# A perceiver block's key tiles on one core: a second buffer for the normed tiles, a batch's first and last tile normed by halves, and another order at a batch's turn

## The reference, cut to what matters

```python
kvx = jnp.einsum('bsi,oi->bso', cond, w_kv_x)       # cond: 8 batches x 1601 rows x 512
kx, vx = jnp.split(kvx, 2, axis=-1)
kx = _ln(kx.reshape(b, sc, g, d), kxln_w, kxln_b)   # g = 8 heads of d = 128, normed each by itself
...
xout = _gqa(qx, kx, vx).reshape(b, s, nh * d)       # softmax(q k^T / sqrt(d)) v
```

## Time and profile before

| | us |
|---|---|
| median of 3 runs | 2889.55 (2889.37 to 2892.36) |
| profiled execution, its time | 2885.77 |
| profiled execution, its span | 2884.0 |
| TensorE busy in the span | 2675.9 (93%) |
| VectorE busy | 1785.2 (62%) |
| ScalarE busy | 1506.5 (52%) |
| GpSimd busy | 465.2 (16%) |
| mean granted TensorE clock | 0.976 |

### The profile page before, as it was taken

How to read it: one execution, slowest core, us unless ns; L and a number is a source line. 1 busy time by engine, 2 the same in 40 slices (tenths; PEclk the granted TensorE clock), 3 DMA queues, 4 the chain that set the end, 5 groups by cost and what they waited for, 6 DMA issues and landing times.

```text
span 2884.0 us, 38434 instructions
## 1 busy us (share of the span) xinstructions
PE 2675.9 (93%) x13446; PEld 2168.4 (75%) x13446; DVE 1785.2 (62%) x4725; ACT 1506.5 (52%) x2919; POOL 465.2 (16%) x376
## 2 busy tenths in 40 slices
PE   6889999999999999999999999989998888969999
PEld 4777787787787787786786777868876778747887
DVE  6748437347356356365374375668668785557997
ACT  6946326235235244244253253446775567846776
POOL 3402002002011011011020020014332222011111
PEclk9999999999999999999999999999999999989999
DMA  3442012021021030030020021435666532529996
GB/s 121 132 154 74 4 45 74 4 60 59 4 71 48 5 89 24 6 94 11 20 85 4 24 86 32 137 117 163 162 183 185 150 76 57 187 90 387 375 372 235
DMA packets 238815, 303.07 MB, mean 105 GB/s; under 512 B 127641, under 2 KB 156953, under 8 KB 225313
## 3 DMA queue, kind: packets, MB, share of 16 engines
q1 hardware_dynamic: 235824, 296.36, 32.3%
q0 software_dynamic: 2800, 4.27, 0.6%
HBM read 259.48 MB, written 46.98 MB: 106 GB/s over the span
## 4 chain that ended last, share of the span: by engine, by line
PE 76%; DVE 11%; ACT 6%; DMA 2%; issue 2%; SPq 1%; POOL 1%; POOLq 0%; DVEq 0%; ACTq 0%
PE ps L103 19%; PE ps L105 19%; PE ps L104 19%; PE ps L753 5%; PE ps L735 3%; PE ps L772 3%; PE ps L802 2%; DVE lnw L1977 1%; DVE zz L1980 1%; DVE cv L1944 1%; PE ps L793 1%; DVE lnw L850 1%; POOL lnw L1099 1%; DMA ca<-cat_d 1%; PE ps L385 1%
## 5 line engine op out<-in xcount | busy, mean ns | idle before, releaser
L1099 POOL TENSOR_TENSOR lnw<-lnw,half 128x8 f32<-128x8 f32 (+1 forms) x104 | 170.9, 1643 | 1417.7 <-DVE lnw L855 1417.7
L103 PE MATMUL ps<-cnh,pth 128*128 128x512 f32 (+1 forms) x832 | 331.8, 399 | 13.6 <-ACT kn L981 13.6
L103 PE MATMUL ps<-whf,cth 128*128 128x512 f32 (+1 forms) x832 | 334.8, 402 | 0.0
L105 PE MATMUL ps<-whf,ctl 128*128 128x512 f32 (+1 forms) x832 | 326.3, 392 | 0.0
L105 PE MATMUL ps<-cnh,ptl 128*128 128x512 f32 (+1 forms) x832 | 326.0, 392 | 0.0
L104 PE MATMUL ps<-cnl,pth 128*128 128x512 f32 (+1 forms) x832 | 325.7, 391 | 0.0
L104 PE MATMUL ps<-wlf,cth 128*128 128x512 f32 (+1 forms) x832 | 325.6, 391 | 0.0
L981 ACT ACTIVATE pr<-ps,lnw 128x128 f32<-128x128 f32 (+1 forms) x384 | 144.2, 456 | 163.8 <-DVE lnw L874 163.8
L2418 DVE TENSOR_TENSOR ml<-mr,mh 128x2048 fp32r<-128x2048 f32 x90 | 203.4, 2287 | 32.2 <-ACT mh L2362 32.2
L971 DVE TENSOR_SCALAR pc<-ps,sm 128x512 f32<-128x512 f32 x64 | 48.1, 751 | 282.1 <-PE ps L105 282.1
L1043 ACT ACTIVATE xo<-ps 128x128 f32<-128x128 f32 x64 | 17.7, 277 | 371.0 <-PE ps L802 371.0
(11 more groups left out here) (331 smaller groups left out, 6086.1 us busy)
## 6 DMA issues: line engine op xcount, KB each, us to landing
mr<-in_moe SPq DMA_DIRECT2D x90, 1024.0 KB, 6.6
ctr<-in_ctxt SPq DMA_DIRECT2D x96, 256.0 KB, 2.9
pr<-in_ctxn SPq DMA_DIRECT2D x96, 256.0 KB
wr<-in_wqkv SPq DMA_DIRECT2D x64, 256.0 KB, 2.9
wvf<-in_wattn SPq DMA_DIRECT2D x12, 1024.0 KB, 4.8
ca<-cat_d SPq DMA_DIRECT2D x16, 512.0 KB, 4.2
qk_d<-cv SPq DMA_DIRECT2D x32, 256.0 KB, 3.2
wr<-in_wz SPq DMA_DIRECT2D x32, 256.0 KB, 3.3
```

The lines of the kernel that those rows point to most:

```text
L103: pe.matmul(dst, lh, rh, start=first, stop=False)
L105: return pe.matmul(dst, ll, rh, start=False, stop=last)
L1099: po.tensor_tensor(rs[0:w, s, :], nv[0:w, s, :], half[0:w, 0:8], ALU.pow).then_inc(kx_rs, 1)
```

## The change

The even tiles of a batch (0, 2, ... 12) are now normed into kn0 and the odd ones into kn (kn_of), and a tile waits for the turn of the tile two before it, tile 0 for that of the last batch's tile 12. Tiles 0 and 12 get their statistics, GpSimd's root and minus mean times root in two halves of four heads: the first half when part 0 of their projection is done (a new semaphore, kx_half), the second when all of it is. In a turn the first four transposes wait for ScalarE's norm alone and the last four for VectorE's.

The lists at a batch's turn are laid anew. TensorE turns tile 10 between the two parts of tile 12's projection; multiplies the first two score pieces before it turns tile 11; projects two chunks of the next tile's part 0, the third score piece, turns tile 12, projects the other two chunks, the last score piece, and part 1. VectorE norms tile 10 ahead of tile 11's statistics, then tile 12's first half of statistics, tile 11's norm, tile 12's second half; the next tile 0's first half of statistics stands before the first reciprocal of the softmax. ScalarE norms tile 12 ahead of writing tile 11's keys.

```diff
+        def in_halves(n):
+            return n % 13 in (0, 12)
+        def kx_half_of(n):
+            return 2 * (n // 13) + 1 + n % 13 // 12
+        def kx_stat_of(n, h):
+            b, i = divmod(n, 13)
+            return 15 * b + (1 + h if i == 0 else i + 2 + (h if i == 12 else 0))
+        def kn_of(n):
+            return kn if n % 13 % 2 else kn0
...
@@ kx_pe @@
                 elif i == 0:
                     pe.wait_ge(kn_ac, n)
-                    pe.wait_ge(kn_dv, n)
...
             for part in parts:
+                if part == 1 and i == 0 and b > 0:
+                    pe.wait_ge(kn_dv, n)
...
+                if part == 0 and chunks[-1] == 3 and in_halves(n):
+                    f.then_inc(kx_half, 1)
@@ kx_turn_pe @@
-            src = kn if i else kn0
-            pe.wait_ge(kn_ac, n + 1)
-            pe.wait_ge(kn_dv, n + 1)
+            src = kn_of(n)
             for p in range(2):
+                pe.wait_ge((kn_ac, kn_dv)[p], n + 1)
@@ s3_pe @@
-                    kx_pe(pe, n)
+                    kx_pe(pe, n, (0,))
+                    if i == 12:
+                        kx_turn_pe(pe, n - 2)
+                    kx_pe(pe, n, (1,))
...
-                    if i > 1:
+                    if 1 < i < 12:
                         kx_turn_pe(pe, n - 2)
+                score_pe(pe, b, 0, 0)
+                score_pe(pe, b, 0, 1)
                 kx_turn_pe(pe, 13 * b + 11)
-                for w in range(3):
-                    score_pe(pe, b, 0, w)
+                if b + 1 < NB:
+                    kx_pe(pe, 13 * b + 13, (0,), (0, 1))
+                score_pe(pe, b, 0, 2)
                 kx_turn_pe(pe, 13 * b + 12)
                 if b + 1 < NB:
-                    kx_pe(pe, 13 * b + 13, (0,), (0, 1))
+                    kx_pe(pe, 13 * b + 13, (0,), (2, 3))
                 score_pe(pe, b, 0, 3)
                 if b + 1 < NB:
-                    kx_pe(pe, 13 * b + 13, (0,), (2, 3))
                     kx_pe(pe, 13 * b + 13, (1,))
@@ kn_free @@
             if i == 0 and b > 0:
-                eng.wait_ge(k_turned, 2 * (n - 13) + 2)
+                eng.wait_ge(k_turned, 2 * (n - 1) + 2)
             elif i == 1 and b > 0:
-                eng.wait_ge(k_turned, 2 * (n - 2) + 2)
                 eng.wait_ge(p_turned, 32 * b - 4)
             elif i > 1:
-                eng.wait_ge(k_turned, 2 * (n - 1) + 2)
+                eng.wait_ge(k_turned, 2 * (n - 2) + 2)
@@ new, called by kx_norm_dv and by the lists @@
+        def kx_nmr_dv(dv, n):
+            dv.wait_ge(kx_rs, kx_stat_of(n, 0))
+            dv.scalar_tensor_tensor(nmr[0:w, s, 0:4], mv[0:w, s, 0:4, 0], -1.0, rs[0:w, s, 0:4],
+                                    ALU.mult, ALU.mult).then_inc(kx_nm, 1)
@@ s3_dv @@
+                    if i == 12:
+                        kx_norm_dv(dv, n - 2)
                     if i > 1:
                         kx_stats_dv(dv, n - 1)
-                    if i > 2:
+                    if 2 < i < 12:
                         kx_norm_dv(dv, n - 2)
-                    split_ctxn_dv(dv, n - 1)
+                    if i < 12:
+                        split_ctxn_dv(dv, n - 1)
...
+                kx_stats_dv(dv, 13 * b + 12, (0,))
                 kx_norm_dv(dv, 13 * b + 11)
-                kx_stats_dv(dv, 13 * b + 12)
+                kx_nmr_dv(dv, 13 * b + 12)
+                kx_stats_dv(dv, 13 * b + 12, (1,))
+                split_ctxn_dv(dv, 13 * b + 11)
                 kx_norm_dv(dv, 13 * b + 12)
...
+                if b + 1 < NB:
+                    kx_stats_dv(dv, 13 * b + 13, (0,))
                 t_rinv = {0: rinv_dv(dv, b, 0)}
                 split_ctxn_dv(dv, 13 * b + 12)
...
                     if g == 0 and b + 1 < NB:
-                        kx_stats_dv(dv, 13 * b + 13)
+                        kx_stats_dv(dv, 13 * b + 13, (1,))
+                        kx_nmr_dv(dv, 13 * b + 13)
@@ s3_ac @@
                 kx_norm_ac(ac, 13 * b + 11)
+                kx_norm_ac(ac, 13 * b + 12)
                 k_out_ac(ac, 13 * b + 11)
-                kx_norm_ac(ac, 13 * b + 12)
                 k_out_ac(ac, 13 * b + 12)
@@ s3_po @@
+                if in_halves(n):
+                    for h in range(2):
+                        po.wait_ge(kx_var, kx_stat_of(n, h))
+                        po.tensor_tensor(rs[0:w, s, 4 * h:4 * h + 4], nv[0:w, s, 4 * h:4 * h + 4], half[0:w, 0:4],
+                                         ALU.pow).then_inc(kx_rs, 1)
```

More of the change, by code:

```diff
@@ L606, in s1b_ac @@
             self_out_ac(ac, 7)
+        kx_half = sem("kx_half")
         kx_done, kx_var, kx_rs, kx_nm = sem("kx_done"), sem("kx_var"), sem("kx_rs"), sem("kx_nm")
@@ L842, in s3_pe, with kx_stats_dv @@
                         xo_pe(pe, m - 1)
-        def kx_stats_dv(dv, n):
+        def kx_stats_dv(dv, n, halves=(0, 1)):
             b, i = divmod(n, 13)
             w, s = TILES[i][1], i % 4
+            lo, hi = 4 * halves[0], 4 * halves[-1] + 4
             src = bank(KSET[i], 2)[0:w, :]
-            dv.wait_ge(kx_done, n + 1)
-            for g in range(8):
+            if halves == (0,):
+                dv.wait_ge(kx_half, kx_half_of(n))
+            else:
+                dv.wait_ge(kx_done, n + 1)
+            for g in range(lo, hi):
                 t = vs(dv.bn_stats(bns[0:w, s, g, :], src[:, 128 * g:128 * g + 128]))
             dv.wait_ge(dv_step, t)
-            for g in range(8):
+            for g in range(lo, hi):
                 t = vs(dv.bn_aggr(mv[0:w, s, g, :], bns[0:w, s, g, :]))
             dv.wait_ge(dv_step, t)
-            dv.tensor_scalar(nv[0:w, s, :], mv[0:w, s, :, 1], 1e-5, None, ALU.add).then_inc(kx_var, 1)
+            dv.tensor_scalar(nv[0:w, s, lo:hi], mv[0:w, s, lo:hi, 1], 1e-5, None, ALU.add).then_inc(kx_var, 1)
         def kn_free(eng, n):
@@ L860, in kn_free @@
             if i == 0 and b > 0:
-                eng.wait_ge(k_turned, 2 * (n - 13) + 2)
+                eng.wait_ge(k_turned, 2 * (n - 1) + 2)
             elif i == 1 and b > 0:
-                eng.wait_ge(k_turned, 2 * (n - 2) + 2)
                 eng.wait_ge(p_turned, 32 * b - 4)
             elif i > 1:
-                eng.wait_ge(k_turned, 2 * (n - 1) + 2)
+                eng.wait_ge(k_turned, 2 * (n - 2) + 2)
+        def kx_nmr_dv(dv, n):
+            i = n % 13
+            w, s = TILES[i][1], i % 4
+            dv.wait_ge(kx_rs, kx_stat_of(n, 0))
+            dv.scalar_tensor_tensor(nmr[0:w, s, 0:4], mv[0:w, s, 0:4, 0], -1.0, rs[0:w, s, 0:4],
+                                    ALU.mult, ALU.mult).then_inc(kx_nm, 1)
         def kx_norm_dv(dv, n):
@@ L871, in kx_norm_dv @@
             src = bank(KSET[i], 2)[0:w, :]
[L872 to L875, removed]
+            dst = kn_of(n)
+            if not in_halves(n):
+                kx_nmr_dv(dv, n)
+            dv.wait_ge(kx_rs, kx_stat_of(n, 1))
             kn_free(dv, n)
@@ L916, in s3_dv @@
         def s3_dv(dv):
-            kx_stats_dv(dv, 0)
+            kx_stats_dv(dv, 0, (0,))
+            kx_stats_dv(dv, 0, (1,))
             split_ctxt_dv(dv, 2)
@@ L923, in s3_dv @@
             dv.wait_ge(self_o, 8)
+            kx_nmr_dv(dv, 0)
             kx_norm_dv(dv, 0)
@@ L976, in kx_norm_ac @@
             src = bank(KSET[i], 2)[0:w, :]
-            dst = kn if i else kn0
+            dst = kn_of(n)
             ac.wait_ge(kx_nm, n + 1)
@@ L1097, in s3_po @@
                 w, s = TILES[n % 13][1], n % 13 % 4
-                po.wait_ge(kx_var, n + 1)
-                po.tensor_tensor(rs[0:w, s, :], nv[0:w, s, :], half[0:w, 0:8], ALU.pow).then_inc(kx_rs, 1)
+                if in_halves(n):
[3 more added lines that the diff above has]
+                                         ALU.pow).then_inc(kx_rs, 1)
+                else:
+                    po.wait_ge(kx_var, kx_stat_of(n, 1))
+                    po.tensor_tensor(rs[0:w, s, :], nv[0:w, s, :], half[0:w, 0:8], ALU.pow).then_inc(kx_rs, 1)
         x = sb("x", [128, 4, 512])
@@ L2025, in program @@
         o_high, o_low, gr_silu = Again(self_exp, 8), Again(self_p, 8), Again(self_turned, 8)
-        og_out, og_turned, gated = Again(kx_var, 104), Again(kx_rs, 104), Again(kx_nm, 104)
+        og_out, og_turned, gated = Again(kx_var, 120), Again(kx_rs, 120), Again(kx_nm, 104)
         ot_high, ot_low, out_done = Again(kx_done, 104), Again(kn_ac, 104), Again(kn_dv, 104)
```

## The result

| | before | after |
|---|---|---|
| median, us | 2890.95 (2889.37 to 2894.64, 4 runs) | 2852.74 (2850.96 to 2854.01, 4 runs) |
| ratio | | 0.9866 (95% interval 0.9848 to 0.9883) |
| profiled execution's span, us | 2884.0 | 2850.2 |

The change makes the kernel 38.2 us faster by the medians, 1.3%. Forecast were 38.6 us and a time of 2851.

The account below looks back on a forecast made before the run. TensorE, busy 93% of the span, bounds the kernel, so only its waits could be won: 33.4 (seven turns) + 2.7 (batch 7) + 2.5 (clock) = 38.6 us off 2889.55, forecast 2851, range 2843 to 2869.

Parts of the forecast that it names:

- The place: Stage 3: TensorE's winnable waits stand at a batch's turn; the second buffer gives nothing in the steady loop.
- The sum of a turn: Tile 12's first matmul to first p v: 21.95 us in place of 26.72, 4.77 less, seven times 33.4.
- The half root: GpSimd's root of half a tile, 4 columns, in a batch's turn: taken as 1.06 us, range up to 1.64.
- The row of 4 columns: GpSimd's root of 4 columns in another stage's trace, 1060 ns, taken as the half root's price.
- the rival at 1.64: A half root costs 1.64 us, as much as 8 columns; 3.57 a turn, time 2859; chance 0.10.
- The first wait: TensorE's wait of 2.50 us before tile 11's turn, laid to the single buffer for normed tiles.
- the wait moves: Only the buffer's 2.50 us a turn goes, later chains end as late: 20 us, time 2869.5; chance 0.12.
- Batch 7: Last batch's turn, without a next tile to fill with: p's transposes at 15.35 for 18.07, 2.7 us less.
- The clock: Shorter TensorE waits mean fewer low-clock stretches: 2.5 us saved of about 5, bounds 0 and 5.
- The slower rival: The clock falls more often, with four more low stretches a turn 8 us slower, 2897; chance 0.03.
- The base: Start of the sum: profiled execution 2885.77 us, giving 2847.2; median 3.8 higher, 2889.55, giving 2851.

Follow-up runs that it names:

- e5: Changed kernel with VectorE's low half of tile 11's context moved behind the norm of tile 12: 2851.62 us, ratio 0.986 to the kernel before.
- e1: Kernel before with only the second buffer for normed tiles added: 2884.17 us, ratio 0.9974 to the kernel before.
- e4: Changed kernel with tile 10's turn put back behind tile 12's whole projection: 2866.73 us, ratio 0.9903 to the kernel before.
- e2: Changed kernel with tiles 0 and 12 normed whole again, not in halves: 2924.62 us, ratio 1.0116 to the kernel before.
- e6: Changed kernel with VectorE's low half of tile 12's context moved behind the next tile 0's norm: 2844.81 us, ratio 0.9836 to the kernel before.
- e3: Changed kernel with one buffer again for tiles 1 to 12: 2867.96 us, ratio 0.9915 to the kernel before.
- e7: Changed kernel with low halves of tile 11's and tile 12's contexts both moved behind later norms: 2846.48 us, ratio 0.9845 to the kernel before.

## Why the prediction was right, and where it was not

- **The place.** Right: the gain is in the turn, and the steady loop gave nothing. A batch less its turn is the same to 0.01 us.
- **The sum of a turn.** Forecast 4.77, measured 4.51; the first p v at t = 22.21 for 21.95. The step that carries most of the error is the second half root of tile 12, priced 1.06 and measured 1.38; e5 takes that away and gains 0.12. The other half roots were 1.00 to 1.01 (1.06 taken). Up to tile 12's turn no step was off by more than 0.2 (tile 11's turn came at 8.34 for 8.5, its end at about 9.2 for 9.4); the last score came at 13.97 for 13.8, since VectorE's late norm stretched that turn and I had taken 1.4 for two chunks that took 1.5; what is left is 0.1 at the first p v.
- **The half root.** The row of 4 columns was the right one, the rival at 1.64 wrong. The rule of the Trainium skill (GPSIMD Engine Reference, Elementwise — side-by-side cycle accounting) of about 2.6 cycles an element does not hold for this power: four columns fewer save 0.6 us.
- **The first wait.** Wrong in what it was laid to. The prediction said that the wait of 2.50 was the single buffer; e1 shows 2.49 with two buffers. It was ScalarE's list (writes of tile 10's keys ahead of the norm) and tile 10's turn behind the whole projection; in the changed kernel the two scores moved ahead fill 1.7 of it and the earlier turn of tile 10 the rest (e4). The sum did not rest on that sentence, since it followed every list step by step. The rival "the wait moves", priced at 7 x 2.5, laid the same 2.50 to the buffer; its price was that of the wait, but the buffer alone brought 0.63 a turn.
- **The parts.** They are not additive. The buffer alone gives 0.6 a turn. Out of the whole change, taking away the buffer costs 1.40, the place of tile 10's turn 1.00, the halves 8.0 and more with the low clock that came with their loss, 6.6 without it (an estimate). The two scores ahead of tile 11's turn, the next tile's two chunks ahead of the third score, and ScalarE's and VectorE's new orders were not run by themselves.
- **Batch 7.** Forecast 15.35 to p's transposes, measured 15.37, with tile 11's keys and the third score at 10.54 for 10.6.
- **The clock.** Forecast 2.5 of 5 saved, bounds 0 and 5; batches 0 to 6 saved all that their low stretches cost, 3.6 from batch 0's first p v on and 0.3 in its turn; batch 7 kept its low stretch. That the total came out within 0.4 us of the forecast is partly luck: the seven turns gave 31.6 for 33.4, and the clock 3.9 for 2.5. The second profile of before shows that the number of stretches varies from run to run (four and six in the turns), so this term has no one value. The slower rival, more low clock, did not come in the changed kernel, but it did in e2.
- **The base.** The sum started from a profiled execution of 2885.77 whose clock at the start was unusual by 5 us. Going over to the median of the runs took that out: 2851 against 2852.74.

## What to carry to other kernels

Follow every engine's list through the stretch, one step after the other, before you name the cause of a wait: the releaser in the profile is the last link, and what holds that link can be another instruction on its own list and not the resource that looks scarce. A buffer, an order and a split into halves can be worth little or a loss alone and much together. After such a change read the next wait the same way: moving one VectorE step of 0.69 us out of the chain that ended last (e6) gave another 0.85 a turn.

## What the runs showed of the hardware

- GpSimd's root is slower beside a VectorE operation that reads two inputs in SBUF: 1.38 against 1.00 for 65 x 4 (changed kernel, e5), 2.01 against 1.63 for 65 x 8 (e2 and the kernel before). Beside VectorE's norm and its low halves of p, whose large input or one of two lies in PSUM, the half roots of the changed kernel took 1.00 and 1.01. The Trainium skill (GPSIMD Engine Reference, Specifications) says that GpSimd shares its SBUF interfaces with VectorE, with contention when a VectorE instruction has two SBUF inputs; e5 agrees, 0.38 us for one such instruction of 0.68.
- TensorE's clock. In batches 0 to 6 of six profiles whose longest wait in a turn was 0.25 to 1.73 us (changed, e3 to e7) there was no low stretch in 42 turns. In three whose waits were 2.5 and 1.95 (before twice, e1) there were twelve in 21 turns. In e2, with a wait of 4.9, every turn had one or two. Batch 7's turn, with its wait of 1.94, had at least one in all ten. That is a count over ten profiles, not an experiment on the clock alone.
- In nine of ten profiles the clock was low for 17.1 us from about 192 to 195 us on, in the one other for 3.4. What tells them apart stays open; of the two profiles of before, the one with the long stretch reaches the first turn 5.9 us later (283.67 against 277.80).
